# Second expert layer of a mixture of experts: four-pass fp32 matmuls replaced by three single-pass ones on high and low parts

## Chip, cores and metric

One core of one Trainium2 chip. The metric is the device time of one execution of the whole program in microseconds; lower is better. Shown is the median over runs of the same kernel.

## What is computed

Two layers of a sequence model on x of shape (1, 2048, 128): a state-space mixer, causal attention with a mixture of experts, a selective scan, and a gated net. The change touches the mixture of experts alone. For each of the 2048 rows nx (normalised), of 8 experts the two with the highest router logits get a weight, all others zero, and every expert is computed for every row:

```python
moe_out = jnp.zeros_like(nx)
for e in range(N_EXPERTS):            # 8
    h = jax.nn.gelu(jnp.einsum('bsd,fd->bsf', nx, fc1_w[e]) + fc1_b[e], approximate=False)   # 128 -> 512
    y = jnp.einsum('bsf,df->bsd', h, fc2_w[e]) + fc2_b[e]                                    # 512 -> 128
    moe_out = moe_out + y * dense_gates[..., e:e + 1]
```

## The kernel before

Everything is float32 in and out, features on partitions, rows along the free axis. Rows are cut into 4 blocks of 512 (`BLK`, `NB`), the hidden 512 into 4 chunks of 128 (`FC`). A **unit** is one expert on one block; the list `UNITS` has 32 of them: experts 0 to 2 on blocks 0 to 2, then on block 3, then expert 3 on all blocks, then, block by block, experts 4 to 7.

Each engine runs its own program in order; semaphores join them. The order within the experts' stage is written by hand, in the loops of `moe_pe`, `moe_act` and `moe_dve`, which count passes k = 0, 1, ..., 33. In pass k:

- TensorE runs `experts_up_pe(k)`, the first layer of unit k, then small chores of other stages, then `experts_down_pe(k - 1)`, the second layer of the unit before. The first layer is done for each chunk by `mm3` (L384), three matmuls of operands in the format float32r, which TensorE takes in one pass: low weights by high inputs, high by low, high by high (L386, L387, L388). The inputs `nx2` and the weights `ew_hi`, `ew_lo` have been split beforehand. Its results go through four PSUM banks (`moe_fill`). The second layer is four matmuls of plain float32 (L1620), each of which stands in the trace as two instructions, weights straight from `ew_raw`, input `hid`; they add up in PSUM bank b over all experts of block b, begun by a matmul of the gates with the second biases (L1616).
- ScalarE applies Gelu to the four chunks of unit k (`experts_act`, L1630), out of PSUM into `hid`, of which there are three.
- VectorE multiplies two chunks at a time by the expert's gate of each row (`experts_dve`, L1638), in place.
- The weights of an expert, 512 KB for both layers, arrive by DMA in one of four slots. ScalarE copies the first layer's half to `ew_hi` (`split_weights_act`, L1643), which rounds it to float32r, and GpSimd subtracts (`split_weights_pool`, in `lo_part`, L652) to make `ew_lo`. The table `SPLIT_AT` says in which pass ScalarE does it. SyncE issues these loads (L1654) and those of the gates' rows (L1666), one for each unit.

Other work is laid between. In passes 0 to 6 it is the rest of attention for the last block and its routing: VectorE's normalisation (L352 to L368), router and top-2 (L1569 to L1596), with a softmax exponential on ScalarE (L1539). From pass 21 on it is the front of the selective scan of block 0 (tables `MF_PE`, `MF_ACT`, `MF_DVE`): residual add (L1707), statistics (L1972), normalised rows (L1904), projections (L1879 to L1896), a convolution on VectorE (L1987), Silu and Softplus on ScalarE (L1939, L1963), each with a table load, and `du` on VectorE (L1998). After a block's last unit `experts_copy_act` takes the sum out of PSUM (L1702), TensorE transposes it (L1695), and VectorE adds it to `x_tok`. After pass 33 comes the scan itself, in which GpSimd makes `drive` (L2055) and VectorE scans (L2077), and then the net.

What waits for what in one unit, in the code's words: `experts_down_pe(n)` waits for `hid_gated >= 2 n + 1` before its chunks 0 and 1, and for `2 n + 2` before chunks 2 and 3.

Of the kernel before, what the change touches and what calls it, by code (L numbers as in the profile page):

```python
# [28 lines left out]
FC = FF // P  # L29
EW_SLOTS, G_SLOTS, HID_SLOTS = 4, 3, 3  # L30

# [64 lines left out]
def build(nc, a):  # L96
# [24 lines left out]
    with ctx:  # L121
# [101 lines left out]
        for bufs, n in ((dt, "dt"), (cs, "cs"), (ecs, "ecs"), (cdec, "cdec"), (bdec, "bdec")):  # L223
# [26 lines left out]
        nx2 = [sb("nx2_hi", [P, T], F32R), sb("nx2_lo", [P, T], F32R)]  # L250
        ew_raw, ew_hi, ew_lo = ([sb(f"ew_{part}0", [P, n, P], dt_)] for part, n, dt_ in
                                (("raw", 2 * FC, F32), ("hi", FC, F32R), ("lo", FC, F32R)))
        MOE_SB_AT = free[0]
# [3 lines left out]
        moe_sb = sb("moe_sb", [P, 2, BLK], F32, at=MOE_SB_AT)  # L257
        assert t_end["moe_sb"] <= free[0]
        gates = sb("gates", [P, TPB, NE], F32)
# [6 lines left out]
        b2 = sb("b2", [NE, D], F32)  # L266
        gate_bc = [sb("gate_bc0", [P, BLK], F32)]
        KZ_HALF = I_END + HA // 2 * T * 2
        assert free[0] <= KZ_HALF, (free[0], KZ_HALF)
        free[0] = KZ_HALF  # L270

        def expert_slot(slot):
            ew_raw.append(sb(f"ew_raw{slot}", [P, 2 * FC, P], F32))
            ew_hi.append(sb(f"ew_hi{slot}", [P, FC, P], F32R))
            ew_lo.append(sb(f"ew_lo{slot}", [P, FC, P], F32R))

        expert_slot(1)
        FRONT_AT = free[0]
        gT = sb("gT", [NE, T], F32, at=t_end["kz"])
        MOE_HIGH = 127232  # L280
        free[0] = MOE_HIGH
        hid = sb("hid", [P, HID_SLOTS, FC, BLK], F32)
        expert_slot(2)
        expert_slot(3)
        assert free[0] >= t_end["probs"]
        gate_bc += [sb(f"gate_bc{n}", [P, BLK], F32) for n in range(1, G_SLOTS)]
        assert free[0] <= A_END, (free[0], A_END)


# [1333 lines left out]

        def experts_act(act, n):
# [8 lines left out]
        def experts_dve(dve, n):  # L1633
            dve.wait_ge(gate_in[n % G_SLOTS], 16 * (n // G_SLOTS + 1))
            for half in range(2):
                dve.wait_ge(S["gelu_done"], FC * n + FC // 2 * (half + 1))
                part = hid[:, n % HID_SLOTS, FC // 2 * half:FC // 2 * (half + 1), :]
                dve.tensor_tensor(part, part, gate_bc[n % G_SLOTS][:, :].unsqueeze(1).broadcast_to([P, FC // 2, BLK]),  # L1638
                                  ALU.mult).then_inc(S["hid_gated"], 1)
# [29 lines left out]
        def moe_sp(sp):  # L1669
# [934 lines left out]
```

## Time and profile before

| | |
|---|---|
| median of 3 runs | 1288.67 us (1288.54 to 1292.73) |
| the profiled execution's own time | 1292.51 us |
| its span, first to last instruction | 1290.7 us |
| TensorE matmul busy | 1147.6 us, 89% |
| VectorE busy | 874.0 us, 68% |
| ScalarE busy | 746.6 us, 58% |
| GpSimd busy | 313.3 us, 24% |
| mean granted clock of TensorE | 0.964 |
| experts' stage | from about 719 to 940 us of the span |

How to read it: PE is TensorE's matmuls, PEld its weight loads, DVE is VectorE, ACT ScalarE, POOL GpSimd, SPq SyncE's DMA queue. L1620 is line 1620 of the kernel. A row of a timeline gives start, length, engine, line, operation, tiles (output first), shapes and the number of instructions merged, and in brackets how long the engine was idle before and who ended that. Matmuls overlap, so a matmul's own length is longer than the distance to the next; starts are the safer reading. The chain of waits follows the program back from its last instruction, at each step to what released it.

### The profile page before, as it was taken

The numbers are of one execution on the slowest core, as the hardware profiler recorded it, in microseconds if no ns is written. First come the engines' busy times: TensorE is split into PE (matmuls) and PEld (weight loads), VectorE is DVE, ScalarE is ACT, GpSimd is POOL, SyncE is SP. The second block draws the span as 40 slices with busy tenths as digits, with TensorE's granted clock in tenths as the row PEclk, the third lists the DMA queues.
The fourth block names the chain that finished last, engine by engine and source line by source line (L and its number), as shares of the span: only waits on it lengthen the run. The fifth ranks groups of instructions, "written<-read, shape, count | busy, mean of one in ns | idle before, by whom it ended". The sixth has DMA issues, their size and how long they took to land.

```text
span 1290.7 us, 15518 instructions
## 1 busy us (share of the span) xinstructions
PE 1147.6 (89%) x5584; PEld 573.3 (44%) x5584; DVE 874.0 (68%) x1660; ACT 746.6 (58%) x1116; POOL 313.3 (24%) x260
## 2 busy tenths in 40 slices
PE   5799777888999999999999999999968889779998
PEld 2455443433333333333322565655523334347776
DVE  4788658958888888878843443444369999964443
ACT  5677532455665565646688544445658676435554
POOL 4323321210010000000011300000079788830000
PEclk9889889999999999989999999999989899889999
DMA  5210553344000000000000312211132223100000
GB/s 163 82 56 29 164 122 82 91 107 92 2 2 2 2 1 1 1 1 2 1 27 10 112 43 60 87 41 33 34 114 107 86 111 115 66 0 1 9 9 17
DMA packets 30491, 67.25 MB, mean 52 GB/s; under 512 B 3816, under 2 KB 16112, under 8 KB 28368
## 3 DMA queue, kind: packets, MB, share of 16 engines
q1 hardware_dynamic: 30416, 66.27, 17.7%
q8 instruction: 45, 0.74, 0.2%
q14 instruction: 30, 0.25, 0.1%
HBM read 57.47 MB, written 8.78 MB: 51 GB/s over the span
## 4 chain that ended last, share of the span: by engine, by line
PE 56%; DVE 15%; POOL 10%; issue 9%; ACT 9%; DMA 1%; SPq 0%; DVEq 0%; POOLq 0%; ACTq 0%
PE psum L1620 8%; PE psum L1328 8%; PE psum L1213 7%; PE psum L1282 6%; POOL drive L2055 6%; DVE mx L1225 6%; PE psum L386 5%; PE psum L388 5%; PE psum L387 5%; DVE hst L2077 2%; ACT probs L1296 2%; ACT psum L2015 1%; ACT edec L615 1%; PE psum L528 1%; PE psum L381 1%
## 5 line engine op out<-in xcount | busy, mean ns | idle before, releaser
L1225 DVE TENSOR_REDUCE mx<-psum 128x1 f32<-128x512 f32 (+3 forms) x640 | 349.2, 604 | 64.7 <-PE psum L1213 35.4
L1296 ACT ACTIVATE probs<-psum 128x1024 f32<-128x1024 f32 (+1 forms) x320 | 283.5, 936 | 171.7 <-PE psum L1282 151.3
L1213 PE MATMUL psum<-kz,qa 128*128 128x512 bf16 (+3 forms) x640 | 199.6, 354 | 22.6 <-DVE mx L1225 16.3
L1282 PE MATMUL psum<-qa,kz 128*128 128x512 bf16 (+1 forms) x640 | 174.9, 361 | 7.2 <-DMA qa<-m_rows 4.2
L1328 PE MATMUL psum<-probs,v 128*32 128x512 f32 (+3 forms) x1280 | 151.3, 544 | 1.5 <-POOL probs L1307 1.4
L1638 DVE TENSOR_TENSOR hid<-hid,gate_bc 128x1024 f32<-128x1024 f32 x64 | 79.0, 1241 | 106.7 <-ACT hid L1630 105.0
L2055 POOL TENSOR_TENSOR drive<-du,b_bc 128x1024 f32<-128x1024 f32 x64 | 148.7, 2359 | 1.4 <-issue 1.4
L2006 PE MATMUL psum<-hst,ident 128*128 128x512 f32 x256 | 122.1, 622 | 21.9 <-DVE u L2095 14.1
L1213 PEld LDWEIGHTS psum<-kz,qa 128*128 128x128 bf16 x640 | 57.1, 97 | 186.1 <-DVE mx L1225 136.9
L1630 ACT ACTIVATE hid<-psum,cols 128x512 f32<-128x512 f32 x128 | 84.7, 689 | 75.5 <-PE psum L388 75.3
L2077 DVE TENSOR_TENSOR_SCAN hst<-psum,hlast,drive 128x512 f32<-128x512 f32 x96 | 115.1, 1263 | 8.4 <-ACT psum L2015 6.4
L1307 POOL TENSOR_SCALAR_AFFINE_SELECT probs<-probs 128x512 f32<-128x512 f32 x48 | 29.4, 636 | 359.4 <-ACT probs L1296 359.4
L1620 PE MATMUL psum<-hid,ew_raw 128*128 128x512 f32 x256 | 115.4, 594 | 0.0
L2015 ACT ACTIVATE psum<-delta 128x1024 f32<-128x1024 f32 x64 | 65.6, 1025 | 55.4 <-DVE hst L2077 55.3
L2006 PEld LDWEIGHTS psum<-hst,ident 128*128 128x128 f32 x256 | 49.1, 198 | 89.8 <-issue 70.2
L1282 PEld LDWEIGHTS psum<-qa,kz 128*128 128x128 bf16 x640 | 57.3, 99 | 66.5 <-ACT probs L1296 26.9
L1620 PEld LDWEIGHTS psum<-hid,ew_raw 128*128 128x128 f32 x256 | 48.0, 189 | 51.5 <-issue 46.2
L652 DVE TENSOR_TENSOR fh_lo<-fh,fh_hi 128x512 fp32r<-128x512 f32 x48 | 32.1, 689 | 56.5 <-ACT fh_hi L2267 56.5
L386 PE MATMUL psum<-nx_hi,ew_lo 128*128 128x512 f32 x128 | 61.3, 479 | 1.0 <-POOL ew_lo L652 1.0
L386 PE MATMUL psum<-fh_hi,fw_lo 128*128 128x512 f32 x144 | 57.2, 398 | 5.4 <-DVE fh_lo L652 5.2
L388 PE MATMUL psum<-fh_hi,fw_hi 128*128 128x512 f32 x144 | 56.2, 390 | 0.0
L387 PE MATMUL psum<-fh_lo,fw_hi 128*128 128x512 f32 x144 | 56.1, 390 | 0.0
(285 smaller groups left out, 1687.8 us busy)
## 6 DMA issues: line engine op xcount, KB each, us to landing
b_bc<-b_rows SPq DMA_DIRECT2D x16, 1024.0 KB, 4.7
cs_bc<-cs_rows SPq DMA_DIRECT2D x16, 512.0 KB, 4.7
gate_bc<-gate_rows SPq DMA_DIRECT2D x32, 256.0 KB, 3.2
qk_part_rows<-qk_parts SPq DMA_DIRECT2D x48, 128.0 KB, 2.3
ew_raw<-experts_dram SPq DMA_DIRECT2D x8, 512.0 KB, 3.6
qa<-qk_part_rows SPq DMA_DIRECT2D x16, 192.0 KB, 5.3
kz<-qk_part_rows SPq DMA_DIRECT2D x16, 192.0 KB, 5.9
fw_raw<-net_dram SPq DMA_DIRECT2D x11, 256.0 KB, 2.7
```

The source lines that it names most:

```text
L386: pe.matmul(out, w[1], x[0], start=start, stop=False, skip_group_check=True)
L387: pe.matmul(out, w[0], x[1], start=False, stop=False, skip_group_check=True)
L388: return pe.matmul(out, w[0], x[0], start=False, stop=stop, skip_group_check=True)
L1213: ins = pe.matmul(out[:, 0:w], qa[:, b, h // 2, i * P:(i + 1) * P], key_rows(h, c)[:, 0:w], start=True, stop=not last, skip_group_check=True)
L1225: dve.tensor_reduce(mx[:, 4 * i + h % 4, c:c + 1], fill_bank("mx", k, n)[:, 0:w], AX.X, ALU.max).then_inc(S["mx_read"], 1)
L1282: ins = pe.matmul(out[:, lo:], key_rows(h, kt // TPB)[:, kt % TPB * P:(kt % TPB + 1) * P], qa[:, b, h // 2, lo:], start=True, stop=not dia ...
L1296: act.activation(probs[:, st % 2, hh, :, lo:], s_pair[n % 2][:, :, lo:], ACT.Exp, scale=SCALE).then_inc(S["p_done"], 1)
L1328: ins = pe.matmul(out[32 * hh:32 * hh + 32, own:], v9[:, at:at + 32], probs[:, st % 2, hh, j, own:], start=(kt == 0), stop=(kt == TPB * (b ...
L1620: ins = pe.matmul(bank[b][:, :], ew_raw[e % EW_SLOTS][:, FC + m, :], hid[:, n % HID_SLOTS, m, :], start=False, stop=(n == block_end[b] and ...
L2006: ins = pe.matmul(bank[j][:, :], ident[:, :], hst[:, (NS1 * b + n) % HBUF, j, :], start=(n == 0), stop=(n == NS1 - 1))
L2055: pool.tensor_tensor(drive[:, k % DRIVE_SLOTS, :, :], du[:, b % 2, :, :], rows.unsqueeze(1).broadcast_to([P, 2, BLK]), ALU.mult).then_inc( ...
L2077: ins = dve.tensor_tensor_scan(hst[:, k % HBUF, j, :], decay[k % 2][:, j, :], drive[:, k % DRIVE_SLOTS, j, :], init, ALU.mult, ALU.add)
```

## The change

The second layer is done like the first, in three single-pass matmuls per chunk. For this its weights are split too, and its input: after the gate product, ScalarE copies `hid` to `hx_hi` (rounded to float32r), and VectorE subtracts to get `hx_lo`, two chunks at a time. Both are done in the same passes as the rest, in an order written out in `moe_act` and `moe_dve`. There are then two buffers of `hid` and two of `hx`, four slots of split weights for both layers, and two of raw weights. A raw slot is free again when its expert is split; a slot of split weights when the last second layer of the expert before it in the slot is done, for which ScalarE's copy waits. GpSimd makes the low weights in two pieces, first layer first. The sums over experts stay in their PSUM banks as before. Some buffers move to other addresses.

```diff
-EW_SLOTS, G_SLOTS, HID_SLOTS = 4, 3, 3
+EW_SLOTS, RAW_SLOTS, G_SLOTS, HID_SLOTS, H_SLOTS = 4, 2, 3, 2, 2
...
+        hx = [sb("hx_hi", [P, H_SLOTS, FC, BLK], F32R), sb("hx_lo", [P, H_SLOTS, FC, BLK], F32R)]
...
-        SPLIT_AT.update({e: last_of[e - EW_SLOTS] + 3 for e in range(EW_SLOTS, NE)})
+        SPLIT_AT.update({e: last_of[e - EW_SLOTS] + 2 for e in range(EW_SLOTS, NE)})
         split_at = {n: e for e, n in SPLIT_AT.items()}
-        load_at = {SPLIT_AT[e]: e for e in range(EW_SLOTS, NE)}
+        load_at = {SPLIT_AT[e - RAW_SLOTS] + 2: e for e in range(RAW_SLOTS + 1, NE)}
...
             if n == first_of[e]:
-                pe.wait_ge(S["ew_split"], 2 * (e + 1))
+                pe.wait_ge(S["ew_split"], 2 * e + 1)
...
+            if n == first_of[e]:
+                pe.wait_ge(S["ew_split"], 2 * (e + 1))
             for m in range(FC):
                 if m % 2 == 0:
-                    pe.wait_ge(S["hid_gated"], 2 * n + m // 2 + 1)
-                ins = pe.matmul(bank[b][:, :], ew_raw[e % EW_SLOTS][:, FC + m, :], hid[:, n % HID_SLOTS, m, :],
-                                start=False, stop=(n == block_end[b] and m == FC - 1), skip_group_check=True)
+                    pe.wait_ge(S["hid_split"], 2 * n + m // 2 + 1)
+                ins = mm3(pe, bank[b][:, :], [w[e % EW_SLOTS][:, FC + m, :] for w in (ew_hi, ew_lo)],
+                          [x[:, n % H_SLOTS, m, :] for x in hx], start=False, stop=(n == block_end[b] and m == FC - 1))
             ins.then_inc(S["down_done"], 1)
...
+        def experts_gelu_act(act, n, half):
             e, b = UNITS[n]
             if n >= HID_SLOTS:
-                act.wait_ge(S["down_done"], n - HID_SLOTS + 1)
-            for m in range(FC):
+                act.wait_ge(S["hid_split"], 2 * (n - HID_SLOTS) + half + 1)
+            for m in range(FC // 2 * half, FC // 2 * (half + 1)):
                 act.wait_ge(S["hid_filled"], FC * n + m + 1)
...
+        def experts_hi_act(act, n, half):
+            if n >= H_SLOTS:
+                act.wait_ge(S["down_done"], n - H_SLOTS + 1)
+            act.wait_ge(S["hid_gated"], 2 * n + half + 1)
+            act.activation(half_of(hx[0], H_SLOTS, n, half), half_of(hid, HID_SLOTS, n, half),
+                           ACT.Copy).then_inc(S["hid_hi"], 1)
...
+        def experts_lo_dve(dve, n, half):
+            dve.wait_ge(S["hid_hi"], 2 * n + half + 1)
+            lo_part(dve, half_of(hx[1], H_SLOTS, n, half), half_of(hid, HID_SLOTS, n, half),
+                    half_of(hx[0], H_SLOTS, n, half)).then_inc(S["hid_split"], 1)
...
         def split_weights_act(act, e):
-            act.wait_ge(slot_in[e % EW_SLOTS], 16 * (e // EW_SLOTS + 1))
-            act.activation(ew_hi[e % EW_SLOTS][:, :, :], ew_raw[e % EW_SLOTS][:, 0:FC, :], ACT.Copy).then_inc(S["ew_split_hi"], 1)
+            act.wait_ge(slot_in[e % RAW_SLOTS], 16 * (e // RAW_SLOTS + 1))
+            if e >= EW_SLOTS:
+                act.wait_ge(S["down_done"], last_of[e - EW_SLOTS] + 1)
+            act.activation(ew_hi[e % EW_SLOTS][:, :, :], ew_raw[e % RAW_SLOTS][:, :, :], ACT.Copy).then_inc(S["ew_split_hi"], 1)
...
             pool.wait_ge(S["ew_split_hi"], e + 1)
+            for layer in (slice(0, FC), slice(FC, 2 * FC)):
+                lo_part(pool, ew_lo[e % EW_SLOTS][:, layer, :], ew_raw[e % RAW_SLOTS][:, layer, :],
+                        ew_hi[e % EW_SLOTS][:, layer, :]).then_inc(S["ew_split"], 1)
...
         def load_weights_sp(sp, e):
-            if e >= EW_SLOTS:
-                sp.wait_ge(S["down_done"], last_of[e - EW_SLOTS] + 1)
+            if e >= RAW_SLOTS:
+                sp.wait_ge(S["ew_split"], 2 * (e - RAW_SLOTS + 1))
...
         def moe_act(o, act):
             for k in range(N_UNITS + 2):
                 if k in split_at:
                     split_weights_act(act, split_at[k])
                 if k < N_UNITS:
-                    experts_act(act, k)
+                    experts_gelu_act(act, k, 0)
+                if 1 <= k <= N_UNITS:
+                    experts_hi_act(act, k - 1, 1)
+                if k < N_UNITS:
+                    experts_gelu_act(act, k, 1)
+                    experts_hi_act(act, k, 0)
...
         def moe_dve(o, dve):
             tail_tok_dve(dve, 15)
             for k in range(N_UNITS + 2):
                 if k < N_UNITS:
-                    experts_dve(dve, k)
+                    experts_gate_dve(dve, k, 0)
+                if 1 <= k <= N_UNITS:
+                    experts_lo_dve(dve, k - 1, 1)
+                if k < N_UNITS:
+                    experts_gate_dve(dve, k, 1)
+                    experts_lo_dve(dve, k, 0)
```

`experts_gate_dve(n, half)` is the gate product of before for one half; `half_of` takes two of the four chunks. In the prediction up(k), down(k), gate(k, half), hi(k, half) and lo(k, half) stand for these functions.

## Rows read from the trace of the kernel before

**Rows 1.** Chain of waits, attention's end and the experts' stage: start, us, what.
```profile
694.67 0.62 ACT ew_hi L1643
...
717.57 1.24 POOL ew_lo L652
...
730.47 0.89 PE psum L1358 x8
...
819.86 3.43 PE psum L1620 x8
826.03 3.43 PE psum L1620 x8
...
890.00 1.72 PE psum L1879 x4
...
932.69 6.88 PE psum L1620 x16
```

**Rows 2.** Timeline of TensorE in one unit of the steady stretch.
```profile
823.36 0.40 PE L387 MATMUL psum<-nx_lo,ew_hi 128*128 128x512 f32 x1
...
825.41 0.39 PE L387 MATMUL psum<-nx_lo,ew_hi 128*128 128x512 f32 x1
```

**Rows 3.** Timelines of ScalarE and VectorE in the same unit.
```profile
824.08 2.67 ACT L1630 ACTIVATE hid<-psum,cols 128x512 f32<-128x512 f32 x4 [3.50 <-PE psum L388]
...
825.50 2.52 DVE L1638 TENSOR_TENSOR hid<-hid,gate_bc 128x1024 f32<-128x1024 f32 x2 [3.65 <-ACT hid L1630]
```

**Rows 4.** Groups by form, 820 to 858 and whole span: busy us, mean ns, idle before.
```profile
L1638 DVE TENSOR_TENSOR hid<-hid,gate_bc 128x1024 f32<-128x1024 f32 x14 | 17.2, 1226 | 26.0 <-ACT hid L1630 25.6
...
L652 DVE TENSOR_TENSOR fh_lo<-fh,fh_hi 128x512 fp32r<-128x512 f32 x48 | 32.1, 689 | 56.5 <-ACT fh_hi L2267 56.5
```

**Rows 5.** Timeline: VectorE's gate products back to back; a subtraction and TensorE in the net.
```profile
757.21 2.36 DVE L1638 TENSOR_TENSOR hid<-hid,gate_bc 128x1024 f32<-128x1024 f32 x2 [3.54 <-ACT hid L1630]
...
1161.13 2.48 DVE L652 TENSOR_TENSOR fh_lo<-fh,fh_hi 128x512 fp32r<-128x512 f32 x4
...
1162.26 0.39 PE L387 MATMUL psum<-fh_lo,fw_hi 128*128 128x512 f32 x1
```

**Rows 6.** Timelines of VectorE, ScalarE and GpSimd in the stage's opening.
```profile
723.15 3.44 DVE L1638 TENSOR_TENSOR hid<-hid,gate_bc 128x1024 f32<-128x1024 f32 x2
...
736.00 3.02 DVE L368 TENSOR_SCALAR xn<-inner,ln_mv,ln_rs 128x128 f32<-128x128 f32 x4
...
750.16 1.28 ACT L1539 ACT_TABLE_LOAD   x1
...
758.89 1.82 POOL L652 TENSOR_TENSOR ew_lo<-ew_raw,ew_hi 128x512 fp32r<-128x512 f32 x1 [20.47 <-ACT ew_hi L1643]
...
759.48 1.28 DVE L1588 SCALAR_TENSOR_TENSOR rank<-rank,ex 128x32 f32<-128x32 f32 x1
```

**Rows 7.** Timelines of VectorE and ScalarE beside the scan's front.
```profile
861.49 0.87 DVE L1972 BATCH_NORM_STATS2 ln_st<-x_tok 128x6 f32<-128x128 f32 x4
...
893.57 2.41 ACT L1630 ACTIVATE hid<-psum,cols 128x512 f32<-128x512 f32 x4
...
897.21 2.73 DVE L1987 SCALAR_TENSOR_TENSOR psum<-cin,cols,psum 128x512 f32<-128x512 f32 x4
...
904.58 1.05 ACT L1942 ACTIVATE sz_even<-sz_even 128x1024 f32<-128x1024 f32 x1
905.65 1.28 ACT L1630 ACT_TABLE_LOAD   x1
...
934.60 1.40 DVE L1998 SCALAR_TENSOR_TENSOR du<-psum,cols,delta 128x512 f32<-128x512 f32 x2
```

**Rows 8.** DMA issues of the page: count, KB each, us to landing.
```profile
ew_raw<-experts_dram SPq DMA_DIRECT2D x8, 512.0 KB, 3.6
```

**Rows 9.** Busy us (count) of PE, PEld, DVE, ACT, POOL in two stretches; PEclk, DMA.
```profile
700.00:720.00 20.00, 17.37 (x119) 4.59 (x118) 2.85 (x11) 16.16 (x20) 3.68 (x5) 1.00 0.09 20
...
940.00:960.00 20.00, 11.76 (x25) 5.20 (x26) 11.50 (x18) 13.32 (x24) 15.59 (x10) 0.74 0.41 158
```

More of the change, by code:

```diff
@@ L250, in build @@
         nx2 = [sb("nx2_hi", [P, T], F32R), sb("nx2_lo", [P, T], F32R)]
-        ew_raw, ew_hi, ew_lo = ([sb(f"ew_{part}0", [P, n, P], dt_)] for part, n, dt_ in
-                                (("raw", 2 * FC, F32), ("hi", FC, F32R), ("lo", FC, F32R)))
-        MOE_SB_AT = free[0]
+        ew_raw, ew_hi, ew_lo = ([sb(f"ew_{part}0", [P, 2 * FC, P], dt_)] for part, dt_ in
+                                (("raw", F32), ("hi", F32R), ("lo", F32R)))
         nx2f = sb("nx2f", [P, BLK], F32)
@@ L256, in build @@
         equal = sb("equal", [P, TPB, NE, NE], F32)
-        moe_sb = sb("moe_sb", [P, 2, BLK], F32, at=MOE_SB_AT)
-        assert t_end["moe_sb"] <= free[0]
+        KZ_HALF = I_END + HA // 2 * T * 2
+        assert free[0] <= KZ_HALF, (free[0], KZ_HALF)
+        free[0] = W_END + 20608
         gates = sb("gates", [P, TPB, NE], F32)
@@ L266, in build @@
         b2 = sb("b2", [NE, D], F32)
-        gate_bc = [sb("gate_bc0", [P, BLK], F32)]
-        KZ_HALF = I_END + HA // 2 * T * 2
-        assert free[0] <= KZ_HALF, (free[0], KZ_HALF)
+        gate_bc = [sb(f"gate_bc{n}", [P, BLK], F32) for n in range(G_SLOTS)]
+        moe_sb = sb("moe_sb", [P, 2, BLK], F32)
+        assert BASE + free[0] <= nc.sbuf_usable_end
         free[0] = KZ_HALF
[L272 to L277, printed above, removed]
+        ew_raw.append(sb("ew_raw1", [P, 2 * FC, P], F32))
+        ew_hi.append(sb("ew_hi1", [P, 2 * FC, P], F32R))
         FRONT_AT = free[0]
         gT = sb("gT", [NE, T], F32, at=t_end["kz"])
-        MOE_HIGH = 127232
+        MOE_HIGH = 107328
         free[0] = MOE_HIGH
         hid = sb("hid", [P, HID_SLOTS, FC, BLK], F32)
[L283 to L286, printed above, removed]
+        hx = [sb("hx_hi", [P, H_SLOTS, FC, BLK], F32R), sb("hx_lo", [P, H_SLOTS, FC, BLK], F32R)]
+        ew_lo.append(sb("ew_lo1", [P, 2 * FC, P], F32R))
+        ew_hi.append(sb("ew_hi2", [P, 2 * FC, P], F32R))
+        ew_lo.append(sb("ew_lo2", [P, 2 * FC, P], F32R))
+        ew_hi.append(sb("ew_hi3", [P, 2 * FC, P], F32R))
         assert free[0] <= A_END, (free[0], A_END)
+        ew_lo.append(sb("ew_lo3", [P, 2 * FC, P], F32R, at=A_END))
+        assert t_end["ew_lo3"] <= W_END
         free[0] = W_END
@@ L336, in build @@
             gT_done gelu_done moe_added nx2_ready lg_filled gates_done gT_filled lgm_done ex8_done ew_split
-            gate_in1 hid_filled slot_in2 down_done hid_gated slot_in3 ew_split_hi gate_in2 moe_copied
+            gate_in1 hid_filled down_done hid_gated ew_split_hi gate_in2 moe_copied hid_hi hid_split
             moe_turned moe_pool_consts in_moe c_in_read c_u_read c_db_read c_dt_read b_saved c_mixed
@@ L1616, in experts_down_pe, with half_of @@
                 pe.matmul(bank[b][:, :], b2[:, :], gT[:, tt], start=True, stop=False, skip_group_check=True)
+            if n == first_of[e]:
+                pe.wait_ge(S["ew_split"], 2 * (e + 1))
             for m in range(FC):
                 if m % 2 == 0:
-                    pe.wait_ge(S["hid_gated"], 2 * n + m // 2 + 1)
-                ins = pe.matmul(bank[b][:, :], ew_raw[e % EW_SLOTS][:, FC + m, :], hid[:, n % HID_SLOTS, m, :],
-                                start=False, stop=(n == block_end[b] and m == FC - 1), skip_group_check=True)
+                    pe.wait_ge(S["hid_split"], 2 * n + m // 2 + 1)
+                ins = mm3(pe, bank[b][:, :], [w[e % EW_SLOTS][:, FC + m, :] for w in (ew_hi, ew_lo)],
+                          [x[:, n % H_SLOTS, m, :] for x in hx], start=False, stop=(n == block_end[b] and m == FC - 1))
             ins.then_inc(S["down_done"], 1)
-        def experts_act(act, n):
+        def half_of(t, slots, n, half):
+            return t[:, n % slots, FC // 2 * half:FC // 2 * (half + 1), :]
+        def experts_gelu_act(act, n, half):
             e, b = UNITS[n]
             if n >= HID_SLOTS:
-                act.wait_ge(S["down_done"], n - HID_SLOTS + 1)
-            for m in range(FC):
+                act.wait_ge(S["hid_split"], 2 * (n - HID_SLOTS) + half + 1)
+            for m in range(FC // 2 * half, FC // 2 * (half + 1)):
                 act.wait_ge(S["hid_filled"], FC * n + m + 1)
@@ L1631, in experts_act @@
                                bias=C("fc1_b", FC * e + m)).then_inc(S["gelu_done"], 1)
[L1633 to L1639, printed above, removed]
+        def experts_hi_act(act, n, half):
[4 more added lines that the diff above has]
+                           ACT.Copy).then_inc(S["hid_hi"], 1)
@@ new lines, in experts_gate_dve @@
+        def experts_gate_dve(dve, n, half):
+            if half == 0:
+                dve.wait_ge(gate_in[n % G_SLOTS], 16 * (n // G_SLOTS + 1))
+            dve.wait_ge(S["gelu_done"], FC * n + FC // 2 * (half + 1))
+            part = half_of(hid, HID_SLOTS, n, half)
+            dve.tensor_tensor(part, part, gate_bc[n % G_SLOTS][:, :].unsqueeze(1).broadcast_to([P, FC // 2, BLK]),
+                              ALU.mult).then_inc(S["hid_gated"], 1)
+        def experts_lo_dve(dve, n, half):
+            dve.wait_ge(S["hid_hi"], 2 * n + half + 1)
+            lo_part(dve, half_of(hx[1], H_SLOTS, n, half), half_of(hid, HID_SLOTS, n, half),
+                    half_of(hx[0], H_SLOTS, n, half)).then_inc(S["hid_split"], 1)
@@ L1645, in split_weights_pool @@
         def split_weights_pool(pool, e):
             pool.wait_ge(S["ew_split_hi"], e + 1)
-            lo_part(pool, ew_lo[e % EW_SLOTS][:, :, :], ew_raw[e % EW_SLOTS][:, 0:FC, :], ew_hi[e % EW_SLOTS][:, :, :]).then_inc(S["ew_split"], 2)
-        slot_in = [sem(f"slot_in{n}") for n in range(EW_SLOTS)]
+            for layer in (slice(0, FC), slice(FC, 2 * FC)):
+                lo_part(pool, ew_lo[e % EW_SLOTS][:, layer, :], ew_raw[e % RAW_SLOTS][:, layer, :],
+                        ew_hi[e % EW_SLOTS][:, layer, :]).then_inc(S["ew_split"], 1)
@@ L1651, in load_weights_sp @@
+        slot_in = [sem(f"slot_in{n}") for n in range(B_SLOTS)]
         def load_weights_sp(sp, e):
-            if e >= EW_SLOTS:
-                sp.wait_ge(S["down_done"], last_of[e - EW_SLOTS] + 1)
-            sp.dma_start(ew_raw[e % EW_SLOTS][:, :, :], a["experts"][e].rearrange("p (j m) -> p j m", m=P)).then_inc(slot_in[e % EW_SLOTS], 16)
+            if e >= RAW_SLOTS:
+                sp.wait_ge(S["ew_split"], 2 * (e - RAW_SLOTS + 1))
+            sp.dma_start(ew_raw[e % RAW_SLOTS][:, :, :], a["experts"][e].rearrange("p (j m) -> p j m", m=P)).then_inc(slot_in[e % RAW_SLOTS], 16)
@@ L1677, in moe_sp @@
             sp.wait_ge(S["pv_done"], step_base[16])
-            for e in range(1, EW_SLOTS):
+            for e in range(1, RAW_SLOTS + 1):
                 load_weights_sp(sp, e)
@@ L1824, in build @@
         b_rows = nc.dram_tensor("b_rows", (NB, NS1, BLK), F32, kind="Internal").ap()
-        B_FROM = 16 * (NE // EW_SLOTS)
+        B_FROM = 16 * (NE // RAW_SLOTS)
         decay = [psum[:, 2:4, :], psum[:, 4:6, :]]
```

## Prediction

> **What bounds the kernel now.** I read the chain of waits first, to see who holds the experts' stage (about 719 to 940 us), then the timelines of one unit, then the places where ScalarE, VectorE or GpSimd has other work. In the steady stretch the chain holds nothing but TensorE: the second layer of one unit starts at 819.86, that of the next at 826.03, so a unit (one expert, one block) takes 6.17 us [rows 1]. Nine passes of the first layer take 825.41 - 823.36 = 2.05 us, 0.228 a pass with its weight load [rows 2]; twelve give 2.74, and the second layer's eight instructions take 3.43 [rows 1]: together 6.17.
>
> Let t be the time since TensorE began a unit's first layer. The pass at 823.36 is the second, so t = 0 is at 823.13. ScalarE starts the four Gelus at t = 0.95 and VectorE the first gate product at 2.37 [rows 3], just as the second Gelu ends. Nothing downstream is late, since the second layer on TensorE runs a unit behind. So the old order hides ScalarE and VectorE completely, and what matters is whether the new order still does.
>
> **What goes.** Per unit the second layer is 12 passes of 0.228 = 2.74 instead of 3.43, so 0.69 less. If TensorE remained the bound, 32 units would give 22 us.
>
> **What comes, and the new loop.** Per unit ScalarE gets two Copies of 128x1024, about 1.05 each (the activation of that size at 904.58 [rows 7]), VectorE two subtractions of 128x1024. A subtraction of 128x512 takes 0.689, the gate product, which also has two inputs, 1.226 for 128x1024 [rows 4]. Below the first a doubled size cannot be, twice the first is 1.38; I take 1.23, the row of the same size. Each engine's sum is below TensorE's 5.48 (ScalarE 4 x 0.66 + 2 x 0.98 = 4.6, VectorE about 4.7). The order is the trouble. In pass k of the loops TensorE runs up(k), then down(k-1), and the second half of down(k-1) now waits for lo(k-1, 1). VectorE issues lo(k-1, 1) behind gate(k, 0), which waits for two Gelus of unit k, which wait for up(k). So the wait is one that TensorE's own current unit feeds:
> - gate(k, 0) starts at t = 2.37, as before [rows 3].
> - lo(k-1, 1) starts 1.14 later: two gate products back to back took 2.36 together, the last of them 1.23 [rows 4, 5]. t = 3.51. Its other input, hi(k-1, 1), sits behind the two Gelus on ScalarE (0.66 from start to start, a quarter of 2.67 [rows 3]) and ends at 2.27 + 1.05 = 3.32, so it is not the later one, by 0.2.
> - It ends at 4.74. From such an end to the first pass is 0.2: the subtraction begun at 1161.13 ends at 1161.82, the second pass behind it starts at 1162.26, the first 0.23 earlier [rows 5]. t = 4.94.
> - Six passes, 1.37: the next unit starts at t = 6.31.
>
> TensorE would reach that half at 2.74 + 1.37 = 4.11, so it stands still for 0.83 per unit. The period is 6.31 against 6.17: **+0.14 for each unit**, +4.3 over the 31 from the first start to the last. With a subtraction of 0.69 it would be 5.77, with 1.38 it is 6.46: from -12 to +9 over 31. The saving is gone, and the loop has no slack: every delay of a Gelu or of VectorE's first two operations of a unit goes into the time. ScalarE goes on with two Gelus and hi(k, 0) and is free from t = 5.6 to the next 0.95 (1.65 us). VectorE goes on with gate(k, 1) and lo(k, 0), which ends at t = 7.0, the next unit's 0.7, and is free to the next 2.37 (1.7 us).
>
> The first half of down(k-1) needs lo(k-1, 0), finished at the next t = 0.7 and wanted at 2.74: covered, by 2 us.
>
> **One-off work against that slack.**
> - Attention's end: the split of expert 0 on ScalarE lies on the chain, 0.62 for 512 elements [rows 1]; 1024 take 1.05: +0.4.
> - Opening, units 0 and 1: gate(0, 0) starts at 723.15 [rows 6]. hi(0, 0) then holds ScalarE until 725.4, the split of expert 1 until 726.4, Gelus of unit 1 until 727.7, and with GpSimd's two subtractions between, gate(1, 0) ends at about 730.4 and lo(0, 1) at 731.6. Down(0) and the attention tail's 0.89 end at 734.1, before at 731.36 [rows 1]: +2.5 beyond the period.
> - Units 2 to 10: four normalisations of the last block, 3.02 in all [rows 6], behind lo(2, 0), and expert 2's split: +2.5. The softmax piece stands on ScalarE between two table loads of 1.28, the first at 750.16 [rows 6], and waits in between for VectorE's routing of some 1.5 behind lo(4, 0): exponential 0.2 and second load end at 3.8 of the next unit, the Gelu is due at 0.95: +2.9. Splits of experts 1 (rest) and 3: +1.0. Against it, TensorE's own chores between up and down (bias matmuls twice more, router, transposes) now fall into its standstill: -2.8. Together +3.6.
> - Experts 4 to 7: the Copy starts at about t = 0.1 (it now waits for the down of the unit before last) and takes 1.05, so Gelus slip by 0.13. GpSimd's two subtractions, 1.24 each [rows 1], from 1.2 to 3.7, cover the moment at which gate(k, 0) wants to start.
>
> What such a meeting costs is seen at 759.48: a VectorE operation on only 128x32 took 1.28 and ended at 760.76, 0.05 after GpSimd's subtraction begun at 758.89 [rows 6]. I take 1.2 + 0.13 for each of four: +5.3; the bounds are 0 (they miss each other) and 2.5 each (both ahead). The Trainium skill, page "SBUF — State Buffer", section "SBUF: two separate sides", calls the port pair of the two engines an exclusive lock held for the whole instruction; by that rule each meeting costs the rest of the other's operation, whole, and this change doubles such operations on both sides. The row at 759.48 agrees [rows 6]; no row shows GpSimd ahead twice running.
>
> - The scan's front, from unit 21. VectorE: the residual add (0.69, as the subtraction of that size [rows 4]), the statistics, 0.87 [rows 7], and their joining, about 0.4: 2.0 behind 0.7, +0.4; the normalised rows, for which TensorE waits, come as much later, and a little more, +0.6; four convolution steps, 2.73 [rows 7], behind 0.7, +1.1. ScalarE: the z part's activations let the Gelu of unit 26 start at 893.57, while TensorE had begun the unit at 890.00 + 1.72 = 891.72 [rows 1, 7]: 1.85 instead of 0.95, +0.9. Unit 27: the Silu waits for a convolution step that is itself behind lo(27, 0) (so t = 7.7); then two activations of 128x512 (1.35), one of 1.05 and a table load of 1.28 [rows 7] let the next Gelu start at 11.4, due at 7.3: +4.1. Unit 29 likewise, with delta's two activations and another table load of 1.28 behind TensorE's part for it: +1.3. Sum +8.4. Before, the unit of lag hid all of this.
> - Tail: the last second layer ended at 932.69 + 6.88 = 939.57 [rows 1], 9.6 after its unit began. Now VectorE has lo(31, 0), 1.40 of du [rows 7] and lo(31, 1) before it: end at t = 11.1. +1.5.
>
> Loads: two raw slots instead of four, and SyncE waits for GpSimd's split of expert e-2 with the gate rows queued behind. Each split comes two or more units (12 us) ahead and a load lands in 3.6 us [rows 8]: no cost. Where it were late, the ScalarE Copy would hold the Gelus.
>
> **Sum**: 0.4 + 4.3 + 2.5 + 3.6 + 5.3 + 8.4 + 1.5 = +26. The scan behind starts only when the stage is over, and nothing later is touched. The profiled execution takes 1292.5 us, 0.3% above the median of 1288.67; 26 on the median gives **1314 us**, +2.0%. No change is within 0.5%.
>
> **Rivals.**
> - TensorE stays the bound, 5.48 a unit. It needs lo(k-1, 1) done 0.83 earlier, at t = 3.9. For it: every engine's sum fits in 5.48. Against: the order of the loops; gate(k, 0) cannot start before two Gelus of the same unit. Price: -22, less up to 9 for unit 27 and the like: 1267 to 1276. This is the case in which the kernel is faster; 8%.
> - Only the period counts and one-off delays overlap or are swallowed: 0.4 + 4.3 + 1.5 = +6, 1295. For it: several of them touch in the same units. 12%.
> - The loop is longer than added up: if the Copy takes over 1.25, hi(k-1, 1) becomes the later input, and GpSimd's meetings double. With 0.3 more a unit and 5 more for meetings: +40, 1329. For it: only 0.2 of margin. 15%.
> - The clock falls. TensorE stands 13% of the time. At 17.37 of 20 us busy it was still at 1.00, at 11.76 it showed 0.74 [rows 9]; so hardly. 3%, beyond 1340.
> - As forecast: 62%.
>
> The range 1296 to 1328 leaves out the first rival, the fourth, and parts of the second and third. Faster 8%, same 7% (half of the second rival), slower 85%.
>
> **What would show it.** In the changed profile, steady units 6.3 apart; a wait of TensorE for VectorE's subtraction of about 0.8 in nearly every unit; VectorE never idle between gate(k, 0) and lo(k-1, 1); the longest unit after number 27. A period near 5.5 with no such wait would prove me wrong, and a wait on ScalarE's Copy ahead of the subtraction would show the third rival.

## The result and the profile after

The changed kernel took 1318.3 us (median of 4 runs, 1313.8 to 1325.1) against 1288.7: a ratio of 1.0227 with a 95% interval of 1.0176 to 1.0277. It is slower, clear of the noise; whether by more than 2% the interval leaves open. Forecast were 1314 and a ratio of 1.020. Five more rounds beside the first experiments gave 1.0226 (1.0198 to 1.0253). Its runs spread over 11 us, those of the kernel before over 4 (in the later rounds 13 against 8); what the traces show of that is told below.

The profiled execution took 1316.5 us, span 1314.7, so 24.0 more span than before. In all that follows lines are those of the changed kernel: its second layer is L384 to L386 with `hx_hi` or `hx_lo` as input, Gelu L1633, gate product L1648, Copy L1640, the subtraction L650. The page's first part:

```profile
PE 1131.3 (86%) x5653; PEld 596.5 (45%) x5712; DVE 950.1 (72%) x1724; ACT 804.5 (61%) x1180; POOL 328.6 (25%) x268
```

TensorE is busy for 16 us less, yet the program is 24 us longer. The chain of waits in the steady stretch says why; it answers to [rows 1], where nothing stood but TensorE:

```profile
830.29 1.34 ACT hid L1633 x2
831.72 1.23 DVE hid L1648
832.94 1.15 DVE hx_lo L650
834.13 0.50 PE psum L384
...
840.40 0.50 PE psum L384
```

Two Gelus of unit k, gate(k, 0), lo(k-1, 1), then TensorE, and round again: the period is 840.40 - 834.13 = 6.27 us (6.29 on the average of this stretch), before 6.17. VectorE's timeline of the same stretch has its four operations without a gap, and its only rest between lo(k-1, 0) and gate(k, 0):

```profile
831.72 1.23 DVE L1648 TENSOR_TENSOR hid<-hid,gate_bc 128x1024 f32<-128x1024 f32 x1 [1.66 <-ACT hid L1633]
832.86 1.22 DVE L650 TENSOR_TENSOR hx_lo<-hid,hx_hi 128x1024 fp32r<-128x1024 f32 x1
833.99 1.22 DVE L1648 TENSOR_TENSOR hid<-hid,gate_bc 128x1024 f32<-128x1024 f32 x1
835.13 1.22 DVE L650 TENSOR_TENSOR hx_lo<-hid,hx_hi 128x1024 fp32r<-128x1024 f32 x1
```

TensorE's timeline around the same wait, with the last pass of the first half, the two passes behind the wait and the first pass of the next unit:

```profile
833.29 0.40 PE L386 MATMUL psum<-hx_hi,ew_hi 128*128 128x512 f32 x1
834.13 0.50 PE L384 MATMUL psum<-hx_hi,ew_lo 128*128 128x512 f32 x1 [0.45 <-DVE hx_lo L650]
834.47 0.40 PE L385 MATMUL psum<-hx_lo,ew_hi 128*128 128x512 f32 x1
...
835.62 0.39 PE L384 MATMUL psum<-nx_hi,ew_lo 128*128 128x512 f32 x1
```

The starts of the two passes around the wait lie 0.84 apart instead of 0.23, so TensorE stood for 0.61 us there; the bracket counts less, since a matmul's own length overlaps the wait.

Who waited for whom in the stage (engine and tile, for whom, total us, times, longest):

```profile
PEld psum L384 <- DVE hx_lo L650: 44.2, 30, 5.0
ACT hid L1633 <- PE psum L386: 40.2, 19, 5.6
PE psum L384 <- DVE hx_lo L650: 31.2, 30, 4.5
```

In these sums, with the same short count for matmuls, TensorE's matmuls waited 31.2 us for the subtraction, 30 times; before, they never waited for VectorE in the whole stage.

Lengths of the passes, read from TensorE's weight-load timelines (start of the first weight load of one unit's first layer to that of the next), us. The stage runs from the first to the start of ScalarE's copy of the last block's sum. The last column is the second profile of the changed kernel (after_again, 1319.3 us).

| | before | changed | difference | forecast | changed, second profile |
|---|---|---|---|---|---|
| units 0 to 10 | 72.7 | 79.7 | +7.0 | +7.6 | 83.1 |
| 11, 12, 13, 17 (a split each) | 24.7 | 30.3 | +5.6 | +5.9 | 30.5 |
| 14 to 16, 18 to 20 | 37.0 | 37.7 | +0.7 | +0.8 | 39.1 |
| 21 to 30 (scan's front) | 75.8 | 86.6 | +10.8 | +9.8 | 87.2 |
| tail from unit 31 | 10.2 | 11.6 | +1.4 | +1.5 | 11.6 |
| stage | 220.5 | 246.0 | +25.5 | +25.6 | 251.5 |

The stage began 1.3 us later, and the scan and the net together were 2.8 us shorter. Over all the profiled executions here, whatever the order of the stage, its start lay between 717 and 725 us and what follows it took 347.5 to 351.2, so neither says anything of the change.

### The profile page after: what moved, and what is told of

Its sections match the earlier page's. It is cut to its first block, busy times and chain, and to the rows that moved or that the text cites. A ratio compares the mean times of both kernels' runs of the same rounds, so it can differ in the third digit from the quotient of the medians.

```text
span 1314.7 us, 15946 instructions
## 1 busy us (share of the span) xinstructions
PE 1131.3 (86%) x5653; PEld 596.5 (45%) x5712; DVE 950.1 (72%) x1724; ACT 804.5 (61%) x1180; POOL 328.6 (25%) x268
## 4 chain that ended last, share of the span: by engine, by line
PE 44%; DVE 23%; ACT 11%; POOL 10%; issue 10%; DMA 1%; SPq 0%; DVEq 0%; ACTq 0%; POOLq 0%
PE psum L1326 7%; DVE mx L1223 7%; PE psum L1211 7%; POOL drive L2084 6%; PE psum L1280 6%; PE psum L384 5%; PE psum L386 4%; PE psum L385 4%; DVE hx_lo L650 4%; DVE hid L1648 3%; ACT hid L1633 2%; DVE hst L2106 2%; ACT probs L1294 2%; PE psum L452 1%; ACT psum L2044 1%
## 5 line engine op out<-in xcount | busy, mean ns | idle before, releaser
L1223 DVE TENSOR_REDUCE mx<-psum 128x1 f32<-128x512 f32 (+3 forms) x640 | 348.9, 603 | 63.5 <-PE psum L1211 30.3
L1211 PE MATMUL psum<-kz,qa 128*128 128x512 bf16 (+3 forms) x605 | 189.9, 351 | 24.7 <-DVE mx L1223 17.3
L1280 PE MATMUL psum<-qa,kz 128*128 128x512 bf16 (+1 forms) x616 | 169.1, 359 | 10.2 <-DMA qa<-m_rows 4.7
L1648 DVE TENSOR_TENSOR hid<-hid,gate_bc 128x1024 f32<-128x1024 f32 x64 | 78.0, 1221 | 64.2 <-ACT hid L1633 64.2
L1633 ACT ACTIVATE hid<-psum,cols 128x512 f32<-128x512 f32 x128 | 82.1, 686 | 40.4 <-PE psum L386 40.2
L650 DVE TENSOR_TENSOR hx_lo<-hid,hx_hi 128x1024 fp32r<-128x1024 f32 x64 | 85.4, 1335 | 0.0
L384 PE MATMUL psum<-hx_hi,ew_lo 128*128 128x512 f32 x128 | 54.7, 427 | 31.2 <-DVE hx_lo L650 31.2
L650 DVE TENSOR_TENSOR fh_lo<-fh,fh_hi 128x512 fp32r<-128x512 f32 x48 | 32.1, 689 | 56.4 <-ACT fh_hi L2296 56.4
L1640 ACT ACTIVATE hx_hi<-hid 128x1024 fp32r<-128x1024 f32 x64 | 67.7, 1058 | 3.0 <-DVE hid L1648 3.0
L384 PE MATMUL psum<-fh_hi,fw_lo 128*128 128x512 f32 x144 | 57.2, 398 | 5.4 <-DVE fh_lo L650 5.2
L1214 PE MATMUL psum<-identb,maskneg 128*128 128x128 bf16 x256 | 55.6, 221 | 1.4 <-DVE mx L1223 1.1
L386 PE MATMUL psum<-fh_hi,fw_hi 128*128 128x512 f32 x144 | 56.1, 390 | 0.0
```

The source lines that it names most:

```text
L384: pe.matmul(out, w[1], x[0], start=start, stop=False, skip_group_check=True)
L386: return pe.matmul(out, w[0], x[0], start=False, stop=stop, skip_group_check=True)
L650: return dve.tensor_tensor(out, value, hi.bitcast(F32), ALU.subtract)
L1211: ins = pe.matmul(out[:, 0:w], qa[:, b, h // 2, i * P:(i + 1) * P], key_rows(h, c)[:, 0:w], start=True, stop=not last, skip_group_check=True)
L1223: dve.tensor_reduce(mx[:, 4 * i + h % 4, c:c + 1], fill_bank("mx", k, n)[:, 0:w], AX.X, ALU.max).then_inc(S["mx_read"], 1)
L1280: ins = pe.matmul(out[:, lo:], key_rows(h, kt // TPB)[:, kt % TPB * P:(kt % TPB + 1) * P], qa[:, b, h // 2, lo:], start=True, stop=not dia ...
```

## The experiments

The changed kernel once more came first, as the base of the three that ran beside it: 

> The changed kernel once more, as the base of the three others on the same chip. Both theories: 1313 to 1325 us, as in its four runs so far, about 1.02 of the kernel before.

1319.1 us (1314.5 to 1327.4), ratio 1.0226.

**lag: the same work in another order.**

```diff
                 if k < N_UNITS:
                     experts_gelu_act(act, k, 0)
-                if 1 <= k <= N_UNITS:
-                    experts_hi_act(act, k - 1, 1)
-                if k < N_UNITS:
                     experts_gelu_act(act, k, 1)
                     experts_hi_act(act, k, 0)
+                    experts_hi_act(act, k, 1)
...
                     experts_gate_dve(dve, k, 0)
-                if 1 <= k <= N_UNITS:
-                    experts_lo_dve(dve, k - 1, 1)
-                if k < N_UNITS:
                     experts_gate_dve(dve, k, 1)
                     experts_lo_dve(dve, k, 0)
+                    experts_lo_dve(dve, k, 1)
```

> Only the order is changed: in each pass ScalarE runs the four Gelus and then both Copies of the same unit, VectorE both gate products and then both subtractions. The work stays the same. Theory (the loop through VectorE's order sets the period): lo(k, 1) ends at 1.8 us of the next unit and is wanted at 4.1, so TensorE never waits, the steady period falls from 6.29 to 5.48 us, the delays behind Silu, Softplus and the convolution are hidden again, and the stage is about 220 - 22 + 1 = 199 us instead of 246: a total of about 1270 us (1264 to 1278), faster than the kernel before. Rival (the engines' capacity sets it: one of them, or the port shared by VectorE and GpSimd, can't do a unit in 5.5): the period stays above 6, total 1300 or more.

Measured 1298.3 us, ratio 1.0053 (1.0034 to 1.0072): 21 us below the changed kernel on the same chip, still not below the one before, and 28 above the 1270 expected, 20 above the upper end. The period did fall as expected: units 15 to 20 took 5.51 to 5.59, and from 826 to 856 us the chain is TensorE alone. So the queue order did set the period of the steady units, and neither the engines' capacity nor the two buffers of `hid` and `hx`, which lag keeps. ScalarE and VectorE do carry a unit without a split in 5.5 us. With splits in three units running it is not always so: units 13 and 14 took 5.95 and 6.81, and the chain there goes through the Copy of the weights and through two gate products that took 3.53 together beside GpSimd, instead of 2.36. The stage took 227.3 us, not 199, so the total came close to the rival's 1300, though for another reason than the rival gives. Most of what was missing lies in three passes, unit 3 with 15.6 us, unit 6 with 12.1 and unit 22 with 10.7. TensorE's timeline in the first of them, with its length behind the start:

```profile
749.26 1.09 PE L379 MATMUL psum<-ident,xn 128*128 128x128 f32 x4 [5.21 <-DVE xn L366]
750.28 2.07 PE L1614 MATMUL psum<-gT,b 8*128 8x512 f32 x2
752.28 0.80 PE L384 MATMUL psum<-hx_hi,ew_lo 128*128 128x512 f32 x1
752.87 0.63 PE L385 MATMUL psum<-hx_lo,ew_hi 128*128 128x512 f32 x1
753.30 0.63 PE L386 MATMUL psum<-hx_hi,ew_hi 128*128 128x512 f32 x1
```

Faster by 0.7 us a unit, TensorE came to the last block's transposes (L379) before VectorE had normalised the rows, and stood 5.2 us. Behind that the passes start 0.43 apart instead of 0.23. The windows of that stretch (columns as in [rows 9]; the clock is the third value from the end):

```profile
740.00:749.00 9.00, 4.05 (x18) 2.97 (x16) 8.91 (x13) 5.38 (x7) 6.90 (x4) 0.99 0.00 0
749.00:757.00 8.00, 7.74 (x20) 5.02 (x21) 5.77 (x7) 2.79 (x3) 0.00 (x0) 0.58 0.81 254
757.00:765.00 8.00, 8.00 (x41) 6.65 (x40) 5.47 (x7) 6.03 (x7) 0.00 (x0) 1.00 0.10 34
```

After 4 of 9 us of work the granted clock is 0.58 on the mean of the next 8 us, so mostly at 1.2 GHz, and back at 2.4 after them. By an estimate from this row the slow stretch costs another 0.42 of 8 us, 3.4, on top of the 5.2.

**lo_first: VectorE's order alone.**

```diff
+                if 1 <= k <= N_UNITS:
+                    experts_lo_dve(dve, k - 1, 1)
                 if k < N_UNITS:
                     experts_gate_dve(dve, k, 0)
-                if 1 <= k <= N_UNITS:
-                    experts_lo_dve(dve, k - 1, 1)
-                if k < N_UNITS:
                     experts_gate_dve(dve, k, 1)
```

> Only VectorE's order is changed: lo(k-1, 1) ahead of gate(k, 0); ScalarE keeps its order, with hi(k-1, 1) behind two Gelus of unit k. Theory: the wait passes from VectorE to ScalarE's order. hi(k-1, 1) ends at 3.32, the subtraction at 4.6, the half at 6.2: period 6.15 to 6.25, 2 to 5 us less in total than the changed kernel, about 1314. Rival (it is gate(k, 0) ahead of the subtraction alone that costs, 1.14 us a unit): period 5.5, total about 1285.

The period is 6.03 us, 0.12 below the least expected and far from the rival's 5.5. Its chain, where VectorE's gate product has gone and ScalarE's Copy stands in its place:

```profile
834.24 0.66 ACT hid L1633
834.90 0.56 issue
835.46 1.06 ACT hx_hi L1640
836.54 1.24 DVE hx_lo L650
```

The total, 1323.7 us (ratio 1.0234, 1.0199 to 1.0268), was not below the changed kernel's 1319.1, where 2 to 5 us less were expected; the ranges of the two overlap. Of the 6.7 us between the two profiled executions (1326.0 and 1319.3), 6.6 lie ahead of the stage, which starts at 723.7 instead of 717.2, and 2.2 behind it; the stage itself is 2.0 shorter, 249.5 against 251.5. Within it unit 22 took 10.9 us instead of 8.3, with a wait of TensorE of 3.7 for the normalised rows, and the tail 12.7 instead of 11.6, which took back most of what the shorter period gave. The theory's mechanism holds for the steady units; its total is not borne out.

**hi_first: ScalarE's order alone.** In the changed kernel `experts_hi_act(act, k - 1, 1)` is moved ahead of `experts_gelu_act(act, k, 0)`; VectorE is as it was.

> Only ScalarE's order is changed against the changed kernel: hi(k-1, 1) ahead of the Gelus of unit k; VectorE keeps gate(k, 0) ahead of lo(k-1, 1). Theory (VectorE's order makes the loop, ScalarE's Copy is ready 0.2 us early): steady period 6.3 as in the changed kernel, within 0.05. Rival (ScalarE's Copy is what comes last): period falls by 0.2 or more.

Steady units took 6.28 us, as the theory says: the Copy is ready early and changes nothing there. (The total is that of a single execution, 1331.4 us: the split units rose from 7.6 to 7.7 to 8.2, and units 26 and 30, beside ScalarE's work for the scan's front, from 7.5 to 9.5 and from 10.9 to 13.5.) Together the two runs place the loop: VectorE's order decides, with ScalarE's 0.2 to 0.3 behind it, and only both together open it.

**one_low_part: the price of GpSimd.**

```diff
-                ins = mm3(pe, bank[b][:, :], [w[e % EW_SLOTS][:, FC + m, :] for w in (ew_hi, ew_lo)],
+                ins = mm3(pe, bank[b][:, :], [ew_hi[e % EW_SLOTS][:, FC + m, :], ew_lo[e % EW_SLOTS][:, m, :]],
...
-            for layer in (slice(0, FC), slice(FC, 2 * FC)):
-                lo_part(pool, ew_lo[e % EW_SLOTS][:, layer, :], ew_raw[e % RAW_SLOTS][:, layer, :],
-                        ew_hi[e % EW_SLOTS][:, layer, :]).then_inc(S["ew_split"], 1)
+            layer = slice(0, FC)
+            lo_part(pool, ew_lo[e % EW_SLOTS][:, layer, :], ew_raw[e % RAW_SLOTS][:, layer, :],
+                    ew_hi[e % EW_SLOTS][:, layer, :]).then_inc(S["ew_split"], 2)
```

> Left out: GpSimd's subtraction for the second layer's weights; the second layer's low weights are read from the first layer's. Price of the meetings of GpSimd and VectorE. Theory (in the four units 11, 12, 13 and 17 with a split, GpSimd's second subtraction holds up VectorE's for its whole length): those units fall from 7.59 to 6.4 us, total 5 to 7 us below the changed kernel, about 1312. Rival (ScalarE's longer Copy of the weights ahead of the Gelus is what costs): they stay at 7.4 or more, total within 1 us of the changed kernel.

1312.4 us, 6.7 below the changed kernel on the same chip; the split units fell from 7.58 to 6.52. In the changed kernel GpSimd's pair and VectorE's subtraction in such a unit were

```profile
801.69 3.54 POOL L650 TENSOR_TENSOR ew_lo<-ew_raw,ew_hi 128x512 fp32r<-128x512 f32 x2 [30.97 <-ACT ew_hi L1660]
...
802.88 1.22 DVE L1648 TENSOR_TENSOR hid<-hid,gate_bc 128x1024 f32<-128x1024 f32 x1 [2.37 <-ACT hid L1633]
804.02 2.30 DVE L650 TENSOR_TENSOR hx_lo<-hid,hx_hi 128x1024 fp32r<-128x1024 f32 x1
```

and with one piece only 1.29 on GpSimd, and 1.26 and 1.15 on the chain for VectorE's two. So VectorE's subtraction lost 1.08, and GpSimd's pair 1.04, 3.54 against the 2.50 of an undisturbed pair (in lag, at 721.26). Here the two engines take turns, a whole operation at a time. The Trainium skill, page "SBUF — State Buffer", section "SBUF: two separate sides", says that whichever of the two starts first holds the ports they share for its whole instruction, and the other waits; these rows agree. The remaining 0.23 of 6.52 over 6.29 goes with ScalarE's Copy of the weights, which stands on the chain of such a unit ahead of the Gelus; that its doubled size alone makes the 0.23 was not tested.

**conv_early: a shorter standstill.** `MF_DVE` gets `26: ("conv0", "conv1")` in place of `26: ("conv0",), 27: ("conv1",)`, in the changed kernel.

> Only the last two convolution steps of the scan's front are moved from VectorE's pass 27 to pass 26 of the changed kernel, so that ScalarE's Silu in pass 27 does not wait for them. Theory (TensorE's standstill of 4.5 us before the second half of down(27) is ScalarE's queue, and the granted clock falls behind it because it is so long): the standstill shrinks to about 2.8 us, the clock stays at 1.00, the unit from 14.1 to about 10.2 us, the one before grows from 7.2 to 8.5. Rival (the clock falls with any standstill there, or for another reason): passes of 0.43 us show again behind it.

Half of it failed. The standstill fell from 4.5 to 2.7 us and the two units took 9.0 and 9.9 us (18.9 in sum, 21.3 in the changed kernel), but the clock fell all the same, if for a shorter time: its mean over the 8 us around the restart is 0.79 (922 to 930), in the changed kernel 0.57 (928 to 936). The total, 1315.1 us in a single execution, lies within the spread of the changed kernel and says nothing. TensorE's timeline of that place:

```profile
922.61 0.50 PE L384 MATMUL psum<-hx_hi,ew_lo 128*128 128x512 f32 x1 [2.66 <-DVE hx_lo L650]
...
923.96 0.63 PE L385 MATMUL psum<-hx_lo,ew_hi 128*128 128x512 f32 x1
924.38 0.63 PE L386 MATMUL psum<-hx_hi,ew_hi 128*128 128x512 f32 x1
```

and three windows around it, where the row in the middle has the clock at 0.57 though TensorE is busy throughout (the columns as in lag's windows above):

```profile
915.00:923.00 8.00, 5.34 (x24) 4.03 (x23) 8.00 (x11) 4.90 (x7) 0.00 (x0) 1.00 0.13 34
923.00:927.00 4.00, 4.00 (x12) 3.14 (x11) 1.82 (x2) 3.71 (x5) 0.00 (x0) 0.57 0.19 66
927.00:935.00 8.00, 6.52 (x25) 4.37 (x25) 4.63 (x4) 5.71 (x9) 0.00 (x0) 1.00 0.09 30
```

**lag_chores and lag_early: what the free order needs.** Both runs have the order of lag. First the chores that TensorE had reached too soon go one pass later:

```diff
-        R3_X, R3_LG, R3_GT = 3, 4, 6
+        R3_X, R3_LG, R3_GT = 4, 5, 7
-        MF_PE = {22: ("turn",), 24: ("x",),
+        MF_PE = {23: ("turn",), 24: ("x",),
...
```

> The order of the run lag, and the last block's routing on TensorE, ScalarE and VectorE one pass later (R3_X, R3_LG, R3_GT = 4, 5, 7), the transposes of the scan's front one pass later on TensorE (pass 23). Theory (in lag TensorE, a unit ahead, reached these chores before VectorE had their inputs, stood 4 to 5 us three times, and its granted clock then fell to 0.5 for some 5 to 10 us): the units of 15.6, 12.1 and 10.7 us fall to 6 to 8, the stage from 227 to 205 to 210 us, total 1275 to 1285, 0.985 to 0.996 of the kernel before. Rival (the order with both halves lagging loses elsewhere, in the splits and the scan's front): total above 1292.

1289.3 us, ratio 0.9988 (0.9971 to 1.0005): even with the kernel before, and above the 1275 to 1285 expected. Units 3, 6 and 22 fell to 6.9, 7.2 and 5.5, but unit 7 rose to 10.7 (3.1 us of wait for the gates, L1524, passes of 0.43 behind it) and unit 24 to 10.8 (a wait of 2.7 for ScalarE's copy). The stage was 218.4, not 205 to 210: the theory named the right kind of loss and not all its places. Then VectorE's chores whose inputs are ready early go ahead of the subtractions (and out of their old place behind them):

```diff
                     experts_gate_dve(dve, k, 1)
+                if k == 2:
+                    route_apply_dve(dve, NB - 1)
+                elif k == R3_LG:
+                    route_top2_dve(o, dve, NB - 1)
+                elif k == R3_GT - 1:
+                    route_gates_dve(o, dve, NB - 1)
+                for part in MF_DVE.get(k, ()):
+                    if part != "stats":
+                        scan_front_dve(o, dve, 0, part)
+                if k < N_UNITS:
                     experts_lo_dve(dve, k, 0)
                     experts_lo_dve(dve, k, 1)
```

> The order of the run lag_chores, with VectorE's normalisation of the last block, its top-2 and gates, the convolution and du put between the gate products and the subtractions of their pass, instead of behind the subtractions. Theory (what is left over TensorE's own sum are chores that reach TensorE late, each with a fall of the clock behind it): TensorE's wait of 3.1 us for the gates goes, and with it the unit of 10.8 us (to about 6.5), the unit with the Silu loses 1 to 2 us; the stage is 209 to 213 us instead of 218, total 1281 to 1287, 0.993 to 0.997 of the kernel before: faster. Rival (the subtractions come late in turn, and TensorE waits for them instead): total 1288 or more.

1283.1 us (1279.7 to 1287.5), ratio 0.9936 (0.9915 to 0.9957): faster than both kernels, the kernel before by 0.6%, the changed one by 2.8%. The stage is 213.1 us; unit 7 took 7.5, unit 28 (behind the Silu) 7.5 instead of 9.7, of which unit 27 gave back 1.3. TensorE's waits in the stage are now

```profile
PE psum L384 <- DVE hx_lo L650: 6.5, 7, 1.7
...
PE psum L1908 <- ACT moe_sb L1721: 2.7, 1, 2.7
```

and unit 3 shows the rival in part: 9.3 us, up from 6.9. The subtractions now wait behind the normalisation, TensorE waits 0.9 for them, and the granted clock is 0.60 over the next 4 us (742 to 746). Unit 24 still takes 10.3.

## Why the prediction was right

- **The loop** (+0.14 a unit): shown. 6.29 against a forecast of 6.31, each stage of it in the chain, and the period moved the way the loop says when either order was changed (6.03, 6.28) or both (5.5). With t counted from TensorE's first pass at 829.34, the gate product starts at 2.38 (forecast 2.37), the subtraction at 3.52 (3.51), the pass behind it at 4.79 (4.94) and the next unit at 6.28 (6.31). Two terms were off and nearly cancel: the step from the subtraction's end to TensorE is 0.04, not 0.2, and the six passes behind the wait take 1.49, not 1.37, since the first of them lasts 0.34 instead of 0.23.
- **TensorE's standstill** of 0.83 a unit: right in kind and place, less in size. By the starts of its passes it is 0.61, with the slow first pass 0.72; the weight loads idle for 0.88 to 0.94.
- **GpSimd's meetings** (+1.33 a unit with a split): 7.57 to 7.59 against 6.29, so +1.29, of which 1.06 went with the second piece. Only the victim differed: not gate(k, 0) but lo(k-1, 1) was held up, and the price is much the same, since both stand in the loop.
- **The opening** (+2.5 and +3.6): in sum +7.0 with the period, forecast 7.6; units 0 and 1 make +3.3 of it (forecast 2.8), units 2 to 10 +3.7 (forecast 4.9). The second profile has +10.3 in sum. The parts were not tested one by one, and the term for chores that fall into the standstill (-2.8) stays an estimate.
- **The scan's front** (+8.4): measured +9.4 beyond the period. Unit 28 alone went from 7.88 to 14.09, +6.2 where +4.1 and +0.14 stood: the gap of 2.0 is about what the clock costs there. The prediction had set its fall aside by the average, 13% of standstill; it did not ask what one long standstill does. Windows of the changed kernel in that unit:

```profile
925.00:930.00 5.00, 0.78 (x4) 0.30 (x2) 2.10 (x2) 4.97 (x8) 0.00 (x0) 0.83 0.00 0
930.00:935.00 5.00, 4.69 (x9) 3.08 (x10) 2.52 (x3) 1.44 (x2) 0.00 (x0) 0.50 0.22 52
```

  Six passes 0.43 apart instead of 0.23 (2.93 on the chain instead of 1.65) and the projection behind them (2.72 instead of 1.72) are about 2.3 us. Against it the statistics and the normalised rows, forecast at +1.0, cost 0.2 beyond the period in units 21 to 25; the convolution and the z part came as forecast (units 26 and 27, +2.0 beyond the period), and delta's activations, forecast at +1.3, cost 1.2 beyond the period in unit 30.
- **The tail** (+1.5): +1.4.
- **Attention's end** (+0.4): the Copy is there with 1.05, but run-to-run shifts of the stage's start by up to 8 us hide it.
- **The loads** (no cost): in the stage no engine waits for a load of weights or gate rows.
- **The rivals.** The engines' sums did fit in 5.5, as the first rival had it, but only in another order, where 6.17 a unit became 5.53. The fourth rival, the clock, came true in part and at another size: not the regular standstills but single stretches brought it down, for some 2 us in unit 28 and more in other units of the second profile.
- **The sum** came out at 26 and the stage's measured excess at 25.5, but so close a match is partly luck: in the second profile of the changed kernel it is 31.1. The medians differ by 29.6, the profiled executions by 24.0, since the one before lay 3.8 above its median and the changed one 1.8 below. So the mechanism and its size hold, and a few us that the falls of the clock bring, in varying number, were not in the sum.

## What to carry to other kernels

When work is put between two stages of a software pipeline, follow the in-order queues once around and add up the loop: busy shares said 5.5 us a unit, the queue order said 6.3. A consumer that runs one unit behind should find everything it waits for queued ahead of anything that needs the producer's current unit. And when a bound engine gets faster, look for the chores placed by hand for its old pace: here, once the loop was open, they cost more than the change gained until they were moved.

## What was not expected of the hardware

- A single standstill of TensorE was mostly followed by a slow stretch: behind the 2.7, 4.5 and 5.2 us shown above the granted clock was 0.50 to 0.58 over 4 to 8 us (passes of 0.43 us instead of 0.23). The nine profiles of the changed kernel and its variants have 26 standstills of 2.4 to 5.5 us in this stage, and 24 of them were followed by 4 us with a mean granted clock of 0.50 to 0.66. Two had not: the changed kernel after 3.04 us at 766, and lag_early after 2.65 us at 873. In their order:

```profile
766.00:770.00 4.00, 3.89 (x17) 3.17 (x18) 3.90 (x7) 2.98 (x5) 2.36 (x2) 1.00 0.02 4
873.00:877.00 4.00, 4.00 (x15) 2.60 (x16) 0.50 (x1) 2.71 (x4) 0.00 (x0) 1.00 0.09 26
```

  So the length of the one standstill does not decide it alone. The regular standstills of 0.6 in every 6.3 us left the clock at 1.00 from 822 to 842 us in both profiles of the changed kernel.
- The same kernel gets the slow stretches in one execution and not in another. In the second profile of the changed kernel the standstill of 3.05 us at 764 was followed by 0.50, and one of 1.77 at 848, in the steady stretch, by 0.66 (unit 18: 7.7 us instead of 6.3), where the first profile has 1.00 behind the same 1.77. The first two rows are those places; the third is the longer stretch, in which the first profile has 1.00:

```profile
766.00:770.00 4.00, 4.00 (x11) 3.13 (x10) 3.04 (x5) 0.69 (x1) 3.07 (x2) 0.50 0.00 0
848.00:853.00 5.00, 4.87 (x14) 3.88 (x15) 2.35 (x3) 0.90 (x2) 0.00 (x0) 0.66 0.16 52
760.00:800.00 40.00, 35.53 (x138) 26.52 (x136) 29.45 (x28) 28.29 (x39) 3.07 (x2) 0.91 0.15 47
```

  Units 3, 5, 6 and 18 took 2.2, 1.0, 0.8 and 1.4 us longer than in the first, about the 5.5 by which its stage is longer. The kernel before, whose TensorE never stood more than 1.0 us at a time in this stage, spread less (8 us over 13 runs against 13 over 6). That the spread of the totals comes from this alone is argued from two profiles, not shown.
- VectorE's operations in its queue started 1.14 us apart though each is 1.22 long, both operations alike, as [rows 5] had suggested.
